# Rows of routed experts gathered by GpSimd instead of loaded by SyncE; shared pieces as three products of rounded parts

## What is computed

```python
scores = jax.nn.softmax(flat @ Wr + router_bias, axis=-1)          # 64 experts
topk_scores, topk_idx = jax.lax.top_k(scores, 4)
topk_scores = topk_scores / topk_scores.sum(-1, keepdims=True)
pos = (jnp.cumsum(oh, axis=0) * oh).sum(-1) - 1                    # place in its expert
valid = pos < CAP                                                  # 128
xb = jnp.zeros((E, CAP, Dx), x.dtype).at[eid, pos].set(flat[tok], mode='drop')
h = jax.nn.silu(jnp.einsum('ecd,edh->ech', xb, Wg)) * jnp.einsum('ecd,edh->ech', xb, Wu)   # H = 128
yb = jnp.einsum('ech,ehd->ecd', h, Wd)
y = yb[eid, jnp.minimum(pos, CAP - 1)] * (w * valid)[:, None]
out = jnp.zeros((N, Dx), x.dtype).at[tok].add(y)
hs = jax.nn.silu(jnp.einsum('nd,sdh->nsh', flat, Sg)) * jnp.einsum('nd,sdh->nsh', flat, Su)  # 2 x 512
out = out + jnp.einsum('nsh,shd->nd', hs, Sd)
```

## Time and profile before

| | |
|---|---|
| median of 3 runs | 1113.02 us |
| the profiled execution | 1115.18 us, span 1113.5 us |
| TensorE busy over the span, mean granted clock | 92%, 0.971 |
| VectorE, ScalarE, GpSimd busy | 65%, 45%, 53% |
| DMA queue of SP (q1), of GpSimd (q0) | 42.6%, 13.1% of 16 engines' span |
| routed experts, first transposes to last y | 837.6 to 1078.9 us |

### The profile page before, as it was taken

The page is one execution under the profiler, slowest core; times in us unless marked ns, Lnnn a source line. Parts: engine busy times, 40 slices in busy tenths (PEclk is TensorE's granted clock), DMA queues, the critical chain, the costliest instruction groups (busy, mean ns, idle before and its releaser), DMA issues. The chain is left out here.

```text
span 1113.5 us, 18851 instructions
## 1 busy us (share of the span) xinstructions
PE 1024.4 (92%) x5364; PEld 738.3 (66%) x5364; DVE 722.2 (65%) x1704; ACT 500.2 (45%) x880; POOL 584.8 (53%) x555
## 2 busy tenths in 40 slices
PE   4999999999879999998899999999999999999960
PEld 2555555565437777775389468577778888888850
DVE  3678778777448888886688248167306666667650
ACT  3666656655238888886432211311304333333320
POOL 6566676674326667665524646356432344333551
PEclk9999999999889999999899999999999999999985
DMA  8467655577645332331540241043269999999729
GB/s 268 151 220 249 205 166 179 192 248 283 240 160 167 104 109 104 103 113 67 185 142 18 91 137 48 11 138 112 87 208 333 337 331 308 288 316 336 190 29 194
DMA packets 128254, 199.49 MB, mean 179 GB/s; under 512 B 35975, under 2 KB 44167, under 8 KB 128186
## 3 DMA queue, kind: packets, MB, share of 16 engines
q1 hardware_dynamic: 106394, 160.40, 42.6%
q0 software_dynamic: 21360, 37.48, 13.1%
q10 hardware_dynamic: 432, 0.79, 0.2%
HBM read 133.10 MB, written 87.56 MB: 198 GB/s over the span
## 5 line engine op out<-in xcount | busy, mean ns | idle before, releaser
L957 POOL TENSOR_TENSOR m_down_lo<-wo,m_down_hi 128x512 fp32r<-128x512 f32 x78 | 129.8, 1684 | 76.3 <-ACT m_down_hi L1053 76.3
L566 PE MATMUL bank<-win,vT 128*128 128x512 f32 x256 | 126.6, 609 | 0.0
L734 DVE TENSOR_REDUCE negmax<-bank 128x1 bf16<-128x512 f32 x128 | 85.6, 672 | 43.3 <-PE bank L573 42.9
L659 ACT ACTIVATE win<-bank 128x512 f32<-128x512 f32 x128 | 69.5, 595 | 92.3 <-PE bank L558 89.9
L1067 DVE TENSOR_TENSOR m_up_lo<-w,m_up_hi 128x1024 fp32r<-128x1024 f32 x78 | 95.5, 1226 | 12.4 <-ACT m_up_hi L1025 11.5
L2075 POOL DMA_INDIRECT out<-m_y,m_token x32 | 51.2, 1600 | 87.1 <-DMA out<-m_y,m_token 47.1
L1304 POOL DMA_INDIRECT tab<-stage_up,slot x64 | 65.6, 1025 | 53.3 <-DVE slot L1650 35.4
L2105 PE MATMUL bank<-y,m_w 128*128 128x128 f32 x736 | 89.7, 275 | 0.0
L2219 ACT ACTIVATE sh_gate_a<-bank 128x512 f32<-128x512 f32 (+1 forms) x40 | 20.5, 512 | 151.4 <-PE bank L2212 121.9
L2075 POOL DMA_INDIRECT sums<-m_y,m_token x32 | 50.6, 1581 | 71.7 <-DVE m_y L2169 41.9
L2105 PEld LDWEIGHTS bank<-y,m_w 128*128 128x128 f32 x736 | 86.4, 193 | 0.1
(11 more groups left out here) (302 smaller groups left out, 2492.8 us busy)
## 6 DMA issues: line engine op xcount, KB each, us to landing
tab<-zeros SPq DMA_DIRECT2D x16, 1056.0 KB
m_w<-in_L_ffn_Wg SPq DMA_DIRECT2D x46, 256.0 KB
m_w<-in_L_ffn_Wu SPq DMA_DIRECT2D x46, 256.0 KB
m_w<-in_L_ffn_Wd SPq DMA_DIRECT2D x46, 256.0 KB
m_x<-tab SPq DMA_DIRECT2D x39, 256.0 KB, 2.7
ytab<-m_y SPq DMA_DIRECT2D x39, 256.0 KB, 2.0
stage_up<-tab SPq DMA_DIRECT2D x32, 264.0 KB
m_x<-tab SPq DMA_DIRECT2D x32, 264.0 KB
```

Source lines behind the costliest of these rows:

```text
L566: nc.tensor.matmul(pO[s * 2 + h][:], vT[:, s, sb_, h:h + 2, :].rearrange("p a c -> p (a c)"), probs[:, sb_ % 2, h, :], start=(sb_ == 0), s ...
L659: nc.scalar.activation(probs[:, b % 2, h, :], pS[h][:], ACT.Exp, scale=1.0 / HEAD).then_inc(p_ready, 1)
L734: nc.vector.tensor_reduce(negmax[:, s, m:m + 1], rough_bank(k, m)[:], AX.X, ALU.max, negate=True).then_inc(pm_read, 1)
L957: nc.gpsimd.tensor_tensor(dn_lo[:, m, :], row(wo0, e * MB + m), dn_hi[:, m, :], ALU.subtract).then_inc(dn_lo_ready, 1)
```

## The change

- SP loads the rows of experts 0 to 7 only. From expert 8 on, the rows are gathered by GpSimd with an indirect DMA, issued right after the scatter of the expert six before. Its indices are `row_at`, the slot's row in `tab1`, or out of bounds where the slot is empty, so empty slots move no row. `row_at` and `empty` are made once from the number of tokens per expert, by a small matmul on `chosen1`. Because an empty slot now keeps whatever the buffer held, the token number is the larger of the row's own and `empty` (NO_TOKEN where empty); it is kept as a float in the table.
- A deferred shared piece is three fp32r matmuls instead of one fp32 matmul. ScalarE rounds `w_sd` (once per chunk, during the first eight pieces) and the hidden piece to high parts, VectorE subtracts to get the low parts, two passes of the loop ahead.
- The SBUF space of `flat_hi`, `flat_lo` and `w_sd` is shared out differently; semaphores are renamed.

```diff
+X_AHEAD = 6
-            nc.gpsimd.iota(zeros[:, D:D + 1].bitcast(I32), [[0, 1]], base=NO_TOKEN, channel_multiplier=1)
+            nc.gpsimd.iota(zeros[:, D:D + 1], [[0, 1]], base=NO_TOKEN, channel_multiplier=1,
+                           allow_small_or_imprecise_dtypes=True)
...
         @block.sync
         def _(sp):
-            for e in range(X_EARLY, X_RING - 1):
+            for e in range(X_EARLY, X_RING):
                 load_rows(sp, T, e)
...
             for i in range(E1 + 1):
-                e = i + X_RING - 1
-                if e < E1:
-                    need(sp, xT_full, i)
-                    need(sp, y_ready, max(i - 1, min(i, 1)))
-                    load_rows(sp, T, e)
                 e = i + W_RING - 1
...
                 if e == JOIN:
-                    pool.wait_ge(back_read, LATE)
+                    pool.wait_ge(back_read, LATE + 1)
...
                     bounds_check=B * SEQ - 1, oob_is_err=False, compute_op=ALU.add).then_inc(added[e % SUMS], 16)
+                n = e + X_AHEAD
+                if X_RING <= n < E1:
+                    pool.wait_ge(back_read, 1)
+                    nc.gpsimd.indirect_dma_start(
+                        row_slot(T, n % X_RING), None, T["tab1"], bass.IndirectOffsetOnAxis(row_at[:, n:n + 1], 0),
+                        bounds_check=E1 * CAP1 - 1, oob_is_err=False).then_inc(rows_in[n % TPB], 16)
...
         @block.tensor
         def _(pe):
+            nc.tensor.matmul(pB[1][:, 0:E1], T["onesb"][:], T["chosen1"][:], start=True, stop=True).then_inc(back_used, 1)
...
-                    pe.wait_ge(loaded[e % W_RING], 64 * (e // W_RING + 1))
+                    pe.wait_ge(*weights_of(e))
+                    if e >= X_RING:
+                        pe.wait_ge(rows_in[e % TPB], 32 * B + 16 * ((e - X_RING) // TPB + 1))
...
-                        last = nc.tensor.matmul(pB[j % 2][:], (late_hidden if j < LATE else hidden)[:, n, tile * P:tile * P + P],
-                                                w_sd[:, n // (HSH // P), n % (HSH // P), :],
-                                                start=(n == 0), stop=(n == CHUNKS - 1))
+                        k, ws, wb, _ = piece(i)
+                        pe.wait_ge(back_lo_ready, k + 1)
+                        for part, (a, w) in enumerate(((back_hi, w_sd_hi), (back_lo, w_sd_hi), (back_hi, w_sd_lo))):
+                            last = nc.tensor.matmul(pB[j % 2][:], a[:, k % 2, :], w[:, ws, wb, :],
+                                                    start=(n == 0 and part == 0), stop=(n == CHUNKS - 1 and part == 2))
+                        last.then_inc(back_used, 1)
...
         @block.scalar
         def _(act):
...
+                    if back_at(i + 2):
+                        k, ws, wb, half = piece(i + 2)
+                        if k < CHUNKS:
+                            nc.scalar.copy(w_sd_hi[:, ws, wb, :], w_sd[:, ws, wb, :])
+                        need(act, back_used, k if k > 1 else 0)
+                        nc.scalar.copy(back_hi[:, k % 2, :], half).then_inc(back_hi_ready, 1)
...
         @block.vector
         def _(dve):
+            dve.wait_ge(back_used, 1)
+            nc.vector.tensor_scalar(empty[:], pB[1][:, 0:E1], T["rowid"][:, 0:1], float(NO_TOKEN), ALU.is_le, ALU.mult)
+            dve.drain()
+            nc.vector.scalar_tensor_tensor(row_at, T["base1"][:], T["rowid"][:, 0:1], empty[:], ALU.add,
+                                           ALU.add).then_inc(back_read, 1)
...
-                    nc.vector.tensor_copy(token[:, m:m + 1], r[:, 0:1].bitcast(I32))
+                    nc.vector.tensor_tensor(token[:, m:m + 1], r[:, 0:1], empty[:, i:i + 1], ALU.max)
...
+                if i < E1 and back_at(i + 2):
+                    k, ws, wb, half = piece(i + 2)
+                    dve.wait_ge(back_hi_ready, k + 1)
+                    if k < CHUNKS:
+                        nc.vector.tensor_tensor(w_sd_lo[:, ws, wb, :], w_sd[:, ws, wb, :], w_sd_hi[:, ws, wb, :], ALU.subtract)
+                    nc.vector.tensor_tensor(back_lo[:, k % 2, :], half, back_hi[:, k % 2, :],
+                                            ALU.subtract).then_inc(back_lo_ready, 1)
```

More of the change, by code:

```diff
@@ L157, in build @@
                 T["hidden"] = T["stage_gate"][:].rearrange("p s (n t) -> p (s n) t", t=SEQ)
+                T["gathered"] = [staged.enter_context(nc.semaphore(f"rows_gathered_{j}")) for j in range(TPB)]
                 T["s_w1"] = [staged.enter_context(nc.semaphore(f"m1_loaded_{n}")) for n in range(W_RING)]
-                T["w_sd"] = sb("w_sd", [P, NSH, DB, HSH], F32, later, "right")
-                T["flat_hi"], T["flat_lo"] = (sb(n, [P, DB, SEQ], F32R, later, "right") for n in ("flat_hi", "flat_lo"))
+                whole = ExitStack()
+                T["w_sd"] = sb("w_sd", [P, NSH, DB, HSH], F32, whole, "right")
+                T["flat_hi"], T["flat_lo"] = (sb(n, [P, DB, SEQ], F32R, whole, "right") for n in ("flat_hi", "flat_lo"))
+                whole.close()
+                T["w_sd_lo"], T["w_sd_hi"] = (sb(n, [P, NSH, DB, HSH], F32R, later, "right") for n in ("w_sd_lo", "w_sd_hi"))
                 splits = ExitStack()
@@ L1195, in middle @@
             "mid_small_loaded", "shared_gate_loaded", "shared_back_loaded"))
-        gathered = [sem(f"y0_gathered_{j}") for j in range(TPB)]
+        gathered = T["gathered"]
         beta_ready, wexp_ready = sem("beta_ready"), sem("wexp_ready")
@@ L2005, in experts @@
         match = sb("m1_match", [P, TOP1])
+        empty, row_at = T["chosen1"], T["base1"][:].bitcast(I32)
+        rows_in = T["gathered"]
         xT = T["y0"][:, TPB - 1].rearrange("p k (b t) -> p k b t", b=DB)
@@ L2013, in experts @@
         h_hi, h_lo = (sb(f"m1_h_{n}", [P, 2, CAP1], F32R) for n in ("hi", "lo"))
+        back_hi, back_lo = (sb(f"shared_back_{n}", [P, 2, P], F32R) for n in ("hi", "lo"))
+        w_sd_hi, w_sd_lo = T["w_sd_hi"], T["w_sd_lo"]
+        back_hi_ready, back_lo_ready, back_used = sem("shared_back_hi_ready"), sem("shared_back_lo_ready"), sem("shared_back_used")
         y = sb("m1_y", [P, RING, D])
@@ L2029, in experts @@
         rest = T["summary"]
-        rest_loaded, joined = sem("rest_loaded"), added[0]
+        rest_loaded, joined = T["out_begun"], added[0]
         block = c.enter_context(nc.Block(no_gpsimd_drain=True))
@@ L2035, in back_at, with weights_of, piece @@
             return divmod(i - BACK, CHUNKS) if 0 <= i - BACK < (LATE + TPB) * CHUNKS else None
+        def weights_of(e):
+            n = e % W_RING
+            return loaded[n], 48 * (e // W_RING + 1) + (16 if n < X_RING else 0)
+        def piece(i):
+            j, n = back_at(i)
+            tile = (AT_ONCE + j) % TPB
+            return i - BACK, n // (HSH // P), n % (HSH // P), (late_hidden if j < LATE else hidden)[:, n, tile * P:tile * P + P]
         def entries(e):
@@ L2110, in _ @@
                         if n == 0:
-                            need(pe, back_read, j - 1)
-                        tile = (AT_ONCE + j) % TPB
-                        last = nc.tensor.matmul(pB[j % 2][:], (late_hidden if j < LATE else hidden)[:, n, tile * P:tile * P + P],
-                                                w_sd[:, n // (HSH // P), n % (HSH // P), :],
-                                                start=(n == 0), stop=(n == CHUNKS - 1))
-                        if n == CHUNKS - 1:
-                            last.then_inc(back_full, 1)
+                            need(pe, back_read, j)
+                        k, ws, wb, _ = piece(i)
[4 more added lines that the diff above has]
+                        last.then_inc(back_used, 1)
                 if valid(i - 1, n=E1):
@@ L2137, in _ @@
                     nc.scalar.activation(g[:, s, :], pH[s][:, 0:CAP1], ACT.Silu).then_inc(g_ready, 1)
-                    act.wait_ge(loaded[i % W_RING], 64 * (i // W_RING + 1))
+                    act.wait_ge(*weights_of(i))
                     need(act, y_full, i - 1)
                     nc.scalar.copy(down_hi[:, s, :], slots[i % W_RING][:, 2, :]).then_inc(down_hi_ready, 1)
+                    if back_at(i + 2):
[4 more added lines that the diff above has]
+                        nc.scalar.copy(back_hi[:, k % 2, :], half).then_inc(back_hi_ready, 1)
         @block.vector
         def _(dve):
+            dve.wait_ge(back_used, 1)
[3 more added lines that the diff above has]
+                                           ALU.add).then_inc(back_read, 1)
             for i in range(E1 + 1):
```

10 lines of the change are left out of this document (5 added, 5 removed).

## The result

The changed kernel takes **1121.06 us** (median of 7 runs, 1117.87 to 1124.99), the kernel before on the same chip 1113.02 us (7 runs, 1111.92 to 1115.11): a ratio of **1.0078, 95% interval 1.0057 to 1.0098**. It is slower by 8.0 us. The profiled execution took 1123.97 us (span 1122.2), 2.9 us above its median.

The account below looks back on a forecast made before the run. The prediction took TensorE to bound the routed experts' stage, with DMA a near bound. Terms -9 + 3 + 8 + 3 + 2 = +7 us took the profiled 1115.18 us to 1122.2, the median to 1120; range 1107 to 1129 us.

Parts of the forecast that it names:

- (a): Shared pieces in the routed experts: three matmuls take 0.70 us against 0.86 us, 56 times, -9.0 us (0 to -12).
- (b): ScalarE's added copies and casts for the pieces: price 0, covered by TensorE.
- (c): VectorE's added subtractions: TensorE has slack, but y and its scatter come up to 2 us later around experts 4 to 10.
- (e) Start: First 15 experts: late scatters and later y make gathers land late, +3 us (0 to +6).
- (e) The addition: Expert 33: scatter 10.7 us late behind the addition, TensorE stalls ahead of expert 39's transposes, +8 us (+4 to +13).
- (e) Behind it: After the stall at the addition: GpSimd still late, seven pairs of experts at 0.44 us, +3 us (0 to +5).
- (e) Clock: Behind the 8 us stall: TensorE runs 4 us at half speed, +2 us (0 to +3).
- (f): Count matmul and indices come once, ahead of the first wait; the tail behind the last y is the same work: 0.
- R1: Faster: queues empty, landings shorten to 4.81 us, the addition takes 7 us, the stall stays 4 us: 1108 us, chance 0.21.
- R2: No net change: stalls of 7 to 11 us in all, 1113 us, chance 0.14.
- R3: The gather loop paces the whole stage, 8.0 us per pair of experts in place of 7.3: 1129 us, chance 0.12.
- R4: Pieces not shortened: weight loads or VectorE hold the step at 3.82 us, stalls remain: 1127 us, chance 0.05.

Follow-up runs that it names:

- e1_pieces: The changed kernel with the rows of experts 8 to 63 loaded whole by SP again, three-matmul pieces kept: 1105.49 us, 0.9973 of the kernel before.
- after_again: The changed kernel, unedited, run again on the chip and in the session of the experiments: 1115.0 us, 1.0074 of the kernel before.
- e10_half: The changed kernel with gathers eight ahead for experts 8 to 40, rows of 41 to 63 loaded whole by SP: 1103.98 us, 0.9970 of the kernel before.
- e7_ahead7: The changed kernel with each gather issued seven experts ahead instead of six: 1110.44 us, 1.0023 of the kernel before.
- e3_ahead8: The changed kernel with each gather issued eight experts ahead instead of six: 1108.26 us, 0.9999 of the kernel before.

## Why the prediction was right

The forecast was 1120.0 us, slower, by the loop of scatter, gather and transposes at the addition; measured were 1121.06. Term by term:

- **(a) The pieces, -9.0.** Right: three matmuls in 0.70 us, a step of 3.66 us, S shorter by 8.6 us over 54 pieces, 8.9 over 56. Neither the third weight load nor VectorE showed.
- **(b), (c) ScalarE and VectorE at nothing.** Right for TensorE. By the windows VectorE is busy 29.92 of 40 us, it was 26.94. The later y of the first experts came: from an expert's transposes to the end of its y are 13.6 to 14.1 us for experts 5 to 9 of e1_pieces, which has no stall, and 12.97 us later on, so up to 1.2 us of the 2 us allowed. Against that, the scatters of 4 to 10 start only 0.8 to 1.9 us behind their y, before 2.9 to 5.6 us: the queue became better than the prediction took it to be.
- **(e) Start, +3.** 3.9 us were measured over experts 8 to 36, 2.0 of them in the 15 experts that the term was for. Not the late scatters that it named made them: the scatters six experts ahead of these waits are 0.8 to 1.5 us late, where scatter 5 was taken to be 4.4. The step that failed is the one landing time for all gathers. Only at expert 13 does the later y of (c) have a part in it, with 1.2 us. That the size came out near is in part luck. Expert 25 shows the step. Its gather and its transposes, from the timelines of GpSimd and TensorE of the kernel after:

```profile
915.74 1.07 POOL L2098 DMA_INDIRECT stage_up<-tab,base  x1 [0.31 <-issue]
```

```profile
923.56 0.72 PE L2123 MATMUL bank<-ident,stage_up 128*128 128x128 f32 x4 [1.41 <-issue]
```

That is 7.8 us from issue to use; the prediction took 4.9 for all of them and had 8.1 only as a bound. The DMA records of this stage put the gathers' landings between about 3 and 7.7 us from issue, half of them within 5 us; some records are missing, so a landing can be later than they say. Of the 9.0 us from y ready to the transposes six experts on (the prediction had 9.1), a scatter 0.8 us behind its y and the 1.89 us from its start to the gather leave 6.3 us for the landing. A gather of 7.7 us overruns that with every scatter on time.
- **(e) The addition, +8.** The idle time was 9.29 us, and 9.45 us of step time. The scatter was 12.5 us late, not 10.7: GpSimd stood 10.95 us idle where the earlier trace rows has 10.09. In the other profile of the changed kernel it stood 8.48 us, scatter 33 was 10.1 us late, and the step was 7.2 us too long: the two lie on both sides of the +8, and whether lighter queues bought anything can't be told from them. The gather, at 4.3 us from issue, was 0.6 us faster than taken. The range of +4 to +13 held both.
- **(e) Behind it, +3.** 3.4 us over experts 44 to 56 (2.6 in after_again). The reason was half right: the scatters ahead of these waits are 1.7 to 2.9 us late, and the gathers take over 5 us. But the 11 us of lateness that the prediction carried on are gone at once: scatter 37 is 0.8 us late again, because TensorE's stall held the next y back.
- **(e) Clock, +2.** 2.8 us at expert 40 (2.3 in after_again): 0.59 granted from 985 to 992 us, 1.28 us for the three piece matmuls in place of 0.70. As in the earlier trace rows, an idle TensorE came back at the 1.2 GHz level.
- **(f) The tail as before.** Right for the change (34.9 against 34.6 us) and wrong as a rule: e1_pieces shows that it held only because the stalls let the scatters catch up. Stalls and tail are one account: the sum -9 + stalls is honest only if the scatters at the end are no later than before. The term was right by luck of the case, not by its reason ("the same work").

Sum: +7 predicted. In the profile after, the same terms are -8.9 + 3.9 + 9.4 + 3.4 + 2.8 = +10.6, with 1.1 us more in small excesses; in that of after_again the stalls are 17.2 us in place of 20.7; by the medians it is 8.0. So the mechanism of the largest term was right, its size between the two profiles, and the agreement to 1 us of the whole is better than the terms deserve. The rivals: R1 needed landings to shorten and the addition to take 7 us; it took 10.95 and 8.48. R2 needed stalls of 7 to 11 us in all, and they came to 20.7 and 17.2. R3 would have needed 8 us per pair all along; the pairs behind expert 8 run at 7.32 us save for the waits listed. R4 falls with the 0.70 us.

On the Trainium skill, "DMA: Bandwidth & Descriptors", "Anatomy of one DMA": its fit gave 2.3 us as an estimate for a gather's flight. The trace disagrees: of the gathers whose records are complete the fastest landed 3.1 us from issue. (With it the sum for the stall at 39 is 10.7 + 1.85 + 2.3 - 9.1 = 5.75 us, not the 5.4 that the prediction names; nothing else hangs on it.)

Left open: why single gathers take 7 us and more, and why the ratio of e10_half does not follow its tail. A table of sums of its own for the deferred tiles, so that no scatter waits for the addition, was not tried.

## What to carry to other kernels

Before an issue moves to another engine's queue, list what blocks in that queue and for how long; here one 10 us wait that had cost nothing became a hole of 7 to 9 us in TensorE. A queue that runs late is a debt that something pays, the next consumer or the end of the kernel, so price a shorter step against the tail as well. Splitting a blocking transfer can cost more than it saves: each of the three parts took half of the wait of the whole. More lead helps by less than the steps it adds when the issuing engine's round becomes as long as the consumer's step, since then its lateness stays.

## What the runs showed of the hardware that was not expected

- **An addition of 256 KB into DRAM kept the next scatter waiting for 4.2 to 5.8 us, one of 768 KB for 8.5 to 11.3 us** (idle time of GpSimd behind the issue, beside SP's loads; three parts in one profile, and the whole in eight: 8.48 in after_again, 11.30 in e7_ahead7, the others 10.09 to 10.95). By the means a third of the bytes costs half of the time.
- **GpSimd's gather stretches beside VectorE's two-input subtraction**: 1.07 to 1.48 us, by the time that was left of the subtraction, and only where the subtraction had begun first. This is read from the 56 gathers of e3_ahead8, with the same pattern in three more traces, and not isolated by a run of its own. By the Trainium skill, "SBUF — State Buffer", "Who interferes with whom", a VectorE instruction with two SBUF inputs contends with a GpSimd instruction that reads SBUF, and the order of issue decides who blocks; the trace agrees. The same section infers that such a subtraction does not hold up the descriptors of a GpSimd DMA; that GpSimd's gather takes 1.48 us here speaks against it, though the trace doesn't show which part of the gather is held up.
- **The start of the stage**, expert 0 to expert 4, lasted 9.2 us in the first two profiles (before and after) and 10.5 to 10.9 us in the eleven of the experiments, on other chips, the unedited change among them; these 1.3 us and more are no effect of an edit, which is why the ruler S begins at expert 4.
